# Attention outputs of three head groups in four copied by ScalarE, divided by GpSimd, and a re-timed order of work

## The reference, cut to what matters

```python
# second layer, causal
scores = jnp.einsum('bhqd,bhkd->bhqk', q, k) / np.sqrt(HEAD_DIM)
scores = jnp.where(causal, scores, -jnp.inf)
attn = jax.nn.softmax(scores, axis=-1)
out = jnp.einsum('bhqk,bhkd->bhqd', attn, v).transpose(0, 2, 1, 3).reshape(b, t, D_MODEL)
return out @ Wo.T
# third layer, two score entries set to -1e9
scores = jnp.einsum('bhqd,bhkd->bhqk', q, k) * scale
scores = scores.at[:, :, 0, -1].set(NEG)
scores = scores.at[:, :, -1, 0].set(NEG)
weights = jax.nn.softmax(scores, axis=-1)
out = jnp.einsum('bhqk,bhkd->bhqd', weights, v)
```

## Time and profile before

| | |
|---|---|
| median of 3 runs | 982.8 us (980.64 to 985.89) |
| the profiled execution | 983.22 us, span 981.6 us |
| PE busy | 876.7 us (89%) |
| DVE busy | 763.0 us (78%) |
| ACT busy | 654.7 us (67%) |
| POOL busy | 354.1 us (36%) |
| chain that ended last | PE 35%, DVE 12%, ACT 5%, issue 3% |

### The profile page before, as it was taken

One profiled execution on the slowest core, in us unless ns is written; L12 is line 12 of the kernel. 1 busy time (PEld: TensorE's weight loads), 2 busy tenths in 40 slices (PEclk: granted clock), 3 DMA queues, 4 the chain that ended last, 5 costly groups with the idle time before them and its releaser, 6 DMA issues.

```text
span 981.6 us, 22916 instructions
## 1 busy us (share of the span) xinstructions
PE 876.7 (89%) x9121; PEld 443.7 (45%) x9127; DVE 763.0 (78%) x1156; ACT 654.7 (67%) x1285; POOL 354.1 (36%) x575
## 2 busy tenths in 40 slices
PE   7999899999878989986889689979989999999985
PEld 5777777778522444443563222326322222222232
DVE  5676676866587778887568599866889999999855
ACT  2556556666336867875556568655778888999972
POOL 1543667567342642235255112432451112111340
PEclk9999999999899999999998999989999999999999
DMA  8000000200501143121420620033106000100000
GB/s 307 1 2 2 1 2 1 76 1 2 155 4 40 35 146 120 37 59 53 120 73 2 189 59 24 12 104 94 53 2 208 21 21 21 38 4 2 5 23 22
DMA packets 49597, 52.52 MB, mean 54 GB/s; under 512 B 9066, under 2 KB 40810, under 8 KB 49332
## 3 DMA queue, kind: packets, MB, share of 16 engines
q1 hardware_dynamic: 45204, 48.12, 16.3%
q0 software_dynamic: 4288, 2.94, 1.1%
HBM read 32.37 MB, written 19.68 MB: 53 GB/s over the span
## 4 chain that ended last, share of the span: by engine, by line
PE 35%; DVE 12%; ACT 5%; issue 3%; DMA 1%; POOL 1%; another core or an unknown queue 1%; DVEq 0%; ACTq 0%; SPq 0%; POOLq 0%
PE banks L1692 12%; PE banks L1657 8%; DVE arena L2031 8%; PE banks L1577 5%; ACT arena L1851 3%; PE banks L1767 2%; PE banks L1775 2%; PE banks L1700 1%; PE banks L1788 1%; PE banks L1715 1%; DMA arena<-arena 1%; ACT arena L1864 1%; DVE arena L2028 0%; PE banks L1811 0%
## 5 line engine op out<-in xcount | busy, mean ns | idle before, releaser
L2031 DVE TENSOR_REDUCE arena<-banks 128x2 f32<-128x1024 f32 (+1 forms) x384 | 441.3, 1197 | 58.0 <-PE banks L1577 28.9
L1851 ACT ACTIVATE arena<-banks 128x512 f32<-128x512 f32 (+1 forms) x768 | 409.8, 588 | 95.4 <-PE banks L1657 64.0
L1692 PE MATMUL banks<-arena 128*9 128x256 f32 (+1 forms) x3328 | 251.2, 381 | 6.7 <-ACT arena L1864 3.9
L1657 PE MATMUL banks<-arena 61*128 61x512 bf16 (+4 forms) x896 | 165.7, 370 | 32.6 <-ACT arena L1851 17.1
L1577 PE MATMUL banks<-arena 56*128 56x512 bf16 (+3 forms) x896 | 163.2, 367 | 20.5 <-DVE arena L2031 15.0
L1657 PEld LDWEIGHTS banks<-arena 61*128 61x128 bf16 (+1 forms) x896 | 44.0, 93 | 192.7 <-ACT arena L1851 157.6
L1433 POOL CAST arena<-arena 16x128 bf16<-16x128 f32 x32 | 9.0, 281 | 293.2 <-ACT arena L1919 283.7
L1692 PEld LDWEIGHTS banks<-arena 128*9 128x9 f32 x3328 | 52.9, 89 | 134.0 <-issue 83.2
L1577 PEld LDWEIGHTS banks<-arena 56*128 56x128 bf16 x896 | 45.2, 95 | 43.4 <-DVE arena L2031 33.3
L414 POOL TENSOR_TENSOR arena<-arena 128x8 f32<-128x8 f32 (+1 forms) x35 | 50.3, 1439 | 30.0 <-DVE arena L2195 27.6
L1443 POOL DMA_DIRECT2D arena<-arena x96 | 55.2, 579 | 10.8 <-POOL arena L1436 9.3
(11 more groups left out here) (241 smaller groups left out, 1398.0 us busy)
## 6 DMA issues: line engine op xcount, KB each, us to landing
arena<-k_products SPq DMA_DIRECT2D x32, 224.0 KB
arena<-q_products SPq DMA_DIRECT2D x64, 112.0 KB
arena<-e_w SPq DMA_DIRECT2D x22, 256.0 KB
q_products<-arena SPq DMA_DIRECT2D x12, 384.0 KB, 3.3
k_products<-arena SPq DMA_DIRECT2D x12, 384.0 KB, 3.9
arena<-arena POOLq DMA_DIRECT2D x96, 4.0 KB, 1.8
sorted_rows<-c_pads SPq DMA_DIRECT2D x2, 709.5 KB, 8.5
q_products<-arena SPq DMA_DIRECT2D x4, 288.0 KB, 3.9
```

What stands on the lines that cost most here:

```text
L1657: ins = nc.tensor.matmul(bank(S_BANK + (use + par) % SCORES)[:, at:at + C - o], Ks[n % NS][rows, y, kt * P:(kt + 1) * P], Qs[n % NS][rows, ...
L1692: ins = nc.tensor.matmul(PS[h * VROWS:h * VROWS + VW, AV_BANK, o:end], V[:, b, kt, HG * g + h, :], Pr[u % PROBS][:, h, o:end], start=(kt = ...
L1851: s_.activation(Pr[s % PROBS][:, 2 * x + par, o:C], scores[:, o:C], ACT.Exp) \
L2031: v_.tensor_reduce(of[:, :, x], two_banks[:, :, 0:width], AX.X, ALU.max).then_inc(ring_dve, 1)
```

## The change

For the first three head groups of each batch and layer (24 of the 32 blocks), the event `O` becomes `Oa`. PE's four transposes stay. ACT copies the 16 x 9 columns from the bank to a new tile `kept`; DVE does nothing. After the third group, a new event `den` has DVE take the reciprocals of all three groups' sums at once (8 times 48 columns), and POOL multiply three groups into `On` (8 times 384 columns). The fourth group keeps the old way. `N` on PE also waits for POOL's multiply. POOL gets one wait more ahead of an early event (`ln3`).

Besides, the table `MOVED` is replaced: about a hundred events move by half a unit to one and a half units against before. A second table moves the scans of units 3, 17, 18, 39 and 125 to 127 by one unit. A third adds two idle matmuls of 512 columns ahead of the first transposes of the experts (`h`, batch 0, tile 4).

```diff
+SCANS_MOVED = {3: -1, 17: 1, 18: 1, 39: 1, 125: 1, 126: 1, 127: 1}
+WARMED = {('h', (0, 4)): 2}
...
+    "H": {(0, 0): 0.5, (0, 1): 0.5, (1, 0): 0.5, (1, 1): 0.5},
...
+    "M": {4: 0.5, 5: -0.5, 7: -0.5, 13: -0.5, 14: -0.5, 15: -1, 21: 0.5, 29: -0.5, 30: -0.5},
...
+        kept, kept_den = A.tile(2, QT, AH - HG, AD + 1), A.tile(2, QT, AH - HG)
...
+        def turned(m):
+
+            return "O" if m // 2 % NG == NG - 1 else "Oa"
...
-                after.setdefault(end + 1 + o_lag, []).append(("O", m))
+                after.setdefault(end + 1 + o_lag, []).append((turned(m), m))
+                if m // 2 % NG == NG - 2:
+                    after.setdefault(end + 2 + o_lag, []).append(("den", (m // 2 // NG, m % 2)))
...
+                    elif kind == "den":
+                        b, c = k
+                        pool.wait_ge(den_ready, 2 * b + c + 1)
+                        g_.tensor_tensor(On[:, QT * c:QT * (c + 1), 0:P - HG * AD].rearrange("p t (h e) -> p t h e", e=AD),
+                                         kept[:, c, :, :, 0:AD],
+                                         kept_den[:, c].unsqueeze(3).to_broadcast([P, QT, AH - HG, AD]),
+                                         ALU.mult).then_inc(on_scaled, 1)
...
+                        pe.wait_ge(on_scaled, 2 * b + c + 1)
...
+                    elif kind == "Oa":
+                        n, c = divmod(k, 2)
+                        b, g = divmod(n, NG)
+                        act.wait_ge(ring_full, place[kind, k] + 1)
+                        if g == 0 and b:
+                            act.wait_ge(on_scaled, 2 * (b - 1) + c + 1)
+                        o4 = bank(ring_bank(place[kind, k])).rearrange("p (t h e) -> p t h e", t=QT, h=HG)
+                        s_.activation(kept[:, c, :, HG * g:HG * (g + 1), :], o4[:, :, :, 0:AD + 1], ACT.Copy) \
+                          .then_inc(ring_act, 1)
...
+                    elif kind == "den":
+                        b, c = k
+                        taken(dve, "Oa", 2 * (NG * b + NG - 2) + c)
+                        ready(dve, on_scaled, 2 * (b - 1) + c + 1)
+                        v_.reciprocal(kept_den[:, c], kept[:, c, :, :, AD]).then_inc(den_ready, 1)
```

More of the change, by code:

```diff
@@ L48 @@
 MOVED = {
-    "D": {1: -0.5},
-    "D17a": {15: 0.5},
-    "D17b": {15: 1},
-    "KS": {2: -0.5, 3: -0.5},
-    "M": {0: 1, 4: 0.5, 15: -1, 20: 0.5, 23: -1, 25: 1},
-    "N": {(0, 0): 0.5},
-    "O": {1: 1, 2: 1, 6: 1, 7: 1, 8: 1, 9: 1, 10: 1.5, 11: 1, 12: 1, 13: 1, 14: 1, 15: 1, 16: 1.5, 17: 1, 18: 1.5,
-        19: 0.5, 20: 1, 24: 1, 25: 1, 26: 1, 27: 1, 28: 1, 29: 1.5, 30: 1},
-    "Ta": {2: -0.5},
-    "Y": {(0, 0): -0.5, (0, 1): -1, (1, 0): -1, (1, 1): -0.5, (2, 0): -0.5, (3, 0): -0.5},
-    "k": {0: -0.5, 1: -0.5, 2: 0.5},
-    "k_part0": {4: -0.5},
-    "k_part1": {5: -1},
-    "k_part2": {5: -1, 7: 1},
-    "k_rem": {4: -0.5},
[14 rows of a table added]
+    "den": {(0, 0): -0.5, (0, 1): -0.5, (2, 0): 0.5, (3, 0): -0.5},
+    "k_part0": {5: 0.5, 6: 0.5, 7: 0.5},
+    "k_part1": {3: -0.5},
+    "k_part2": {2: 1, 3: -0.5, 7: 1},
+    "k_rem": {3: -0.5},
     "lat": {3: 1},
-    "ln": {3: 0.5},
+    "ln": {2: -0.5},
     "ln3": {3: 0.5},
-    "q": {0: -0.5, 1: -1},
-    "q_part0": {2: 0.5, 3: 0.5},
-    "q_part1": {3: 1, 5: -1},
-    "q_part2": {2: 0.5, 3: 0.5, 5: -0.5, 6: 0.5, 7: 1.5},
-    "q_rem": {4: -0.5},
-    "scale": {0: -1},
-    "split": {0: 0.5, 4: 0.5, 15: -1, 23: -1},
-    "square": {(0, 0): 0.5, (1, 0): -1},
-    "v": {1: -0.5, 2: 1, 3: 1},
-    "warm": {6: 0.5},
-    "x": {(0, 0): 0.5, (0, 1): 0.5, (0, 2): 0.5},
-    "xs3": {3: -1},
-}
+    "put": {(1, 1): -0.5, (1, 2): -0.5},
+    "q": {0: -0.5},
+    "q_part0": {2: 0.5, 6: 0.5, 7: 0.5},
+    "q_part1": {4: -0.5},
+    "scale": {2: 0.5, 3: 1},
+    "split": {4: 1.5, 5: -0.5, 7: -0.5, 15: -1, 21: 0.5, 27: 1, 29: -0.5},
+    "square": {(0, 0): 0.5, (1, 0): -1, (1, 1): 1},
+    "stat": {(1, 0): -0.5, (1, 1): -0.5},
+    "warm": {2: 0.5, 6: 1},
+    "x": {(0, 2): -0.5},
+}
+SCANS_MOVED = {3: -1, 17: 1, 18: 1, 39: 1, 125: 1, 126: 1, 127: 1}
+WARMED = {('h', (0, 4)): 2}
 SORTED = NT + NE - 1
@@ L389, in build @@
                                          "k_full", "k_part0", "k_rem", "k_part1", "k_part2")}
+        den_ready, on_scaled = sem("denominators_inverted"), sem("first_groups_scaled")
         counts = {}
@@ L1091, in scanned, with lead_of @@
         def scanned(u):
+            return lead_of(u) + SCANS_MOVED.get(u, 0)
+        def lead_of(u):
             if u < AHEAD:
@@ L1200, in order @@
                           ("warm", 20), ("Ta", 3), ("warm", 2), ("P", 3), ("R", 3)]
-        RINGED = "A M O N Y W T Ta P H G C x h y D k q v T0 Q QS lat KL K KS V0".split()
-        BY_ACT, BY_BOTH = "M H x k q Ta T0 Q QS lat KL K KS V0".split(), "h"
+        RINGED = "A M O Oa N Y W T Ta P H G C x h y D k q v T0 Q QS lat KL K KS V0".split()
+        BY_ACT, BY_BOTH = "M Oa H x k q Ta T0 Q QS lat KL K KS V0".split(), "h"
         ring = [e for e in order() if e[0] in RINGED]
@@ L1417, in _ @@
                     elif kind == "ln3":
+                        pool.wait_ge(av_cleared, 1)
                         t = slice(QT * k, QT * (k + 1))
@@ L1539, in _ @@
                             pe.wait_ge(o_kept if q >= 2 else g_silu, NTILE)
+                        warm(bk, WARMED.get((kind, k), 0))
                     if kind == "D16a":
@@ L1642, in _ @@
                             pe.wait_ge(exp_done, exps_of[use + 1 - SCORES])
+                        warm(bank(S_BANK + use % SCORES), WARMED.get((kind, k), 0))
                         if x == 0 and kt == 0:
@@ L1696, in _ @@
                             ins.then_inc(av_done, 1)
-                    elif kind == "O":
+                    elif kind in ("O", "Oa"):
                         pe.wait_ge(o_copied, k + 1)
```

2 lines of the change are left out of this document (1 added, 1 removed), and 11 rows, old and new, of the table MOVED.

## The result

| | before | after |
|---|---|---|
| median | 981.5 us | 973.3 us (969.9 to 977.9) |
| ratio | | 0.991, 95% interval 0.9892 to 0.9929 |
| profiled execution | 983.2 us, span 981.6 | 972.5 us, span 970.7 |
| mean granted clock of it | 0.975 | 0.981 |

The change makes the kernel 0.9% faster, 8.2 us by the medians. The two profiled executions differ by 10.9 us of span, and a part of that is not the change: over 40 executions of the kernel before on the same chip, the mean granted clock of TensorE went from 0.966 to 0.985, and the times at these two ends are 987.4 and 975.8 us, 6.1 us for each 0.01; a straight line fitted through all 40 gives 5.7. By these slopes the 0.006 between the two profiles go along with 3.4 to 3.7 us.

A forecast was written before the change was run, and what follows sets the result against it. DVE was taken as nearly full in 280 us behind the retention, PE close behind. DVE -5.3, ACT +2.0, moves -4.2 and reload +1.1 gave -6.4 from 983.2: 976.8 us, likeliest 972 to 979, 8-in-10 range 968 to 986.

The forecast's parts named there:

- DVE's relief: At the 24 `O` taken off DVE, 0.61 us each: -2.2, -2.1 and -1.0 us on the path.
- ACT's price: 24 copies of 0.37 us on ACT: +1.0 us in blocks 24 to 28, +1.0 us at the other 19 places.
- `den` on DVE: Eight new reciprocals of 48 columns at 0.27 us each give 2.2 us of work back to DVE.
- GpSimd's product: Eight new 384-column products on POOL, at most 1.27 us each: nothing on the path, even with a split queued behind.
- The moved events: Waits at block 0's start, `KL` 2, block 5, `H` and block 25, 6.35 us together: two thirds go, -4.2 us.
- the prediction's own sign of being wrong: Wrong if the waits turn up again one event later, or if unpriced moves carry more than 3 us.
- The rest: The other moves and the later scans 125 to 127: taken as zero, with 3 us to either side.
- The reload: `q_part2` 5 half a unit later, so PE's 2.26 us wait for the reload at 553.64 grows: +1.1 us.
- no change: PE and ACT take over from DVE and waits return at the next event: 982 us, chance 0.25.
- All of it: DVE's 12.4 us count nearly in full and the moved events' waits go: 970 us, chance 0.12.
- ACT in the loop: All 24 copies delay the exponentials, 8.9 us on the path, hiding DVE's relief: 989 us, chance 0.10.
- POOL against DVE: Eight POOL products each hold one DVE instruction by 1.4 us, 11.4 us in all: 988 us, chance 0.03.

The follow-up runs named there:

- Experiment 4: Changed kernel, with DVE given a 16-column reciprocal and a 128-column sum at each of the 24 copied outputs: 972.54 us, ratio 0.9918.
- experiment 5: Changed kernel, with ScalarE doing each of the 24 copies twice, the first into an unread tile: 971.82 us, ratio 0.9904.
- Experiment 1: Changed kernel's new `O` with the old table of moves, no moved scans, no idle matmuls: 988.75 us, ratio 1.0081 to the kernel before.
- experiment 6: Kernel of experiment 1 with two `den` later, behind splits 22 and 31 (the second also behind block 29's copy): 982.87 us, ratio 1.0025.
- experiment 3: Kernel before, old `O`, with only the moves that the prediction priced: 980.21 us, ratio 0.9992.
- experiments 2: Changed kernel's table, moved scans and idle matmuls, but every `O` the old way on DVE: 975.77 us, ratio 0.9944.
- experiment 7: Kernel before, old `O`, with the new table's 57 changed entries ahead of unit 96, scans 3, 17, 18, 39 moved, and idle matmuls: 973.75 us, ratio 0.9928.
- experiment 10: Kernel before with four table entries changed around unit 76 (`O` 11, `M` 13, `M` 14, `scale` 0): ratio 0.9977, on another chip.
- experiment 8: Kernel of experiment 1 with idle matmuls on PE in the two waits for splits, blocks 22 and 31: 989.55 us, ratio 1.008.
- e9: Changed kernel with `q_part2` 7 (the last reload) one and a half units later: ratio 0.9902, 959.4 us beside 970.4 on another chip.
- e12: Kernel before, old `O`, with the 29 changed entries ahead of unit 28 and moved scans 3, 17, 18: ratio 0.9961, on another chip.

## Why the prediction came near, and where its steps failed

The time, 973.3 us, lies 3.5 us under the forecast of 976.8 and inside its range. The mechanism was wrong, and the sum came near by luck: wrong terms cancelled.

*DVE's relief, -5.3 us in three terms: nothing that can be measured.* Experiment 4 gives DVE the time back at no cost. The step that failed is the reading of the earlier trace rows. The wait of 0.34 us ahead of the scan product was charged to the `O`. Its releaser is a scan, and that scan stands ahead of the reciprocal in DVE's queue. DVE's scans and the reciprocal behind them, in the kernel before (PE's weight load follows at 850.17):

```profile
847.77 2.35 DVE L2031 TENSOR_REDUCE arena<-banks 128x2 f32<-128x1024 f32 x2
...
850.04 0.25 DVE L2043 RECIPROCAL arena<-banks 128x16 f32<-128x16 f32 x1
```

The same place in the kernel after, without any `O` on DVE:

```profile
838.27 2.35 DVE L2068 TENSOR_REDUCE arena<-banks 128x2 f32<-128x1024 f32 x2
...
840.24 0.30 ACT L1949 ACTIVATE arena<-banks 128x144 f32<-128x144 f32 x1 [0.27 <-PE banks L1727]
...
840.67 0.10 PEld L1603 LDWEIGHTS banks<-arena 56*128 56x128 bf16 x2 [0.34 <-DVE arena L2068]
...
841.17 1.23 DVE L2068 TENSOR_REDUCE arena<-banks 128x2 f32<-128x1024 f32 x1 [0.55 <-PE banks L1608]
```

The wait is 0.34 us again, and the half unit 1.37 us again (840.24 to 841.61), not 1.14 to 1.3. DVE now stands idle 0.55 us where it did the `O` before. A stretch in which DVE works 97% of the time can still have room where the instruction stands.

*ACT's price, +2.0 us: nothing that can be measured* (experiment 5). The same rows show the copy starting in ScalarE's idle time. Its length was 0.30 us, between 0.27 and 0.60 as bounded, under the 0.37 taken, and the next instruction starts before it ends (840.42 here, 0.18 us behind the copy's start). The Trainium skill's figure ("VectorE: DVE Perf Modes", the section on the TRN2 errata) gave an estimate of 0.26 us; the measured 0.30 is nearer to it than to the row that the prediction took.

*`den` on DVE* took 0.45 us, not 0.27: two rows of 16 and 128 columns don't price a reciprocal of 48. 3.6 us of DVE instead of 2.2, hidden.

*GpSimd's product, nothing on the path: right only for the new table.* The step named the mishap ("behind it in POOL's queue can stand a block's split, which would be late by 1.3 us at most") and priced it at nothing, as the DMAs had several units. Experiment 1 measured 1.2 us late and 2.54 us of waiting, since the late DMAs fell in with the reload, and two places with what followed cost 5.9 us by the medians (7.7 us in units 128 to 222 of the two profiles, experiment 6). The new table puts split 22 and the copy of block 29 ahead of their `den`. The structure and its table had to be priced together.

*The moved events, -4.2 us for five named waits: the sign right, the reason short.* In the kernel after 5.2 us net of the 6.35 are gone, and at `KL` 2 the prediction's own sign of being wrong is there: the wait turned up again one event later, 1.17 us ahead of `K` 2. The named moves alone brought 0.8 us (at most 2.8, experiment 3). *The rest "zero, with 3 us to either side"* was the larger term: the start as a whole brings 3.8 us, `O` 11 and its neighbours another 2.2, and the whole table 5.5 to 7.1 (experiments 2 and 7), so the unpriced moves carry more than 3 us. The wait of 2.88 us at 517.18 is longer than any of the earlier trace rows and was not among them, though the diff moves `O` 11. And waits were priced by their length alone, without the clock behind them.

*The reload, +1.1 us: wrong in sign.* PE's wait for it went from 2.26 to 0.55 us, with 1.40 us for a split just ahead of it, 1.95 together, where 3.4 was expected.

Of the rivals, *no change* and *all of it* both rested on DVE. *All of it* also has its sum wrong: it says that DVE's 12.4 us count nearly in full and puts in 8; with 12.4 it would be 965.5 us, outside its own 966 to 972. *ACT in the loop* fell by experiment 5. *POOL against DVE* didn't occur at the new product. One line on the 32 merges of the kernel after and one on the eight products, durations in ns as least, median and most:

```profile
L2075 DVE TENSOR_TENSOR arena<-arena x32: 175/176/1041, 265.8 to 915.3; 128x16 f32<-128x16 f32 x32
```
```profile
L1448 POOL TENSOR_TENSOR arena<-arena x8: 849/854/1164, 374.0 to 916.0; 128x384 f32<-128x384 f32 x8
```

The three long merges lie beside other two-tile instructions of GpSimd (at 353.11, 434.83 and 504.65 us); the one long product, at 525.66, lies beside DVE's product of `q_rem`. So instructions of the two engines take longer side by side, as the earlier trace rows showed, and either engine can be the one held, but no merge met the new product. The merge reads two SBUF tiles, as in the rule that the prediction cites from the Trainium skill ("GPSIMD Engine Reference", section 8), and this trace agrees: up to 1.04 us beside GpSimd instead of 0.18.

## What to carry to other kernels

Before crediting an instruction with a wait, look where the releaser stands in its queue: work that stands behind the releaser can be taken away at no gain, however full the engine. Put the old cost back by itself: one run that gave DVE its work back told more than the sum of all DVE's terms. When an operation is split over a second engine, list what stands behind each new wait on that engine, DMAs that feed another engine first, and price structure and order together.

## What the runs showed of the hardware

The place of PE's idle time counts, not only its sum. Behind a wait of 2.88 us at 517 us and one of 2.54 us at 754 us the granted clock was 0.50 for 5 us and more, and work took up to 1.94 us instead of 1.12; behind a single wait of 1.53 us at 746.7 us half units stayed at 1.12. Cut in two (experiment 10) or filled with idle matmuls (experiment 8), the wait left the clock at 1.00. But the same wait at the same place can go either way. Behind the 1.39 us that PE waits for a scan at 717.96 us in the kernel before and at 711.30 in experiment 7, the windows are:

```profile
718.00:721.00 3.00, 3.00 (x33) 1.21 (x35) 2.90 (x7) 1.31 (x3) 1.30 (x4) 1.00 0.00 0
711.00:714.00 3.00, 2.70 (x17) 1.09 (x19) 1.93 (x4) 0.29 (x2) 0.36 (x2) 0.54 0.00 0
```

So one profile doesn't tell whether a wait costs the clock. The spread of the kernel before from run to run, 975.8 to 988.0 us, goes along with the mean granted clock.

The three DMAs of split 22 had landed 4.8 us after the first was issued when the reload came 1.2 us behind them (experiment 6), and 5.9 to 6.1 us after it when the reload was issued in the same moment (experiment 1 and the kernel after). Those of split 31, with no reload beside them, took 3.1 us (experiment 1). On another chip the kernel before took 970.4 us instead of 981, and the stages that were shorter there are two beside the experts, units 96 to 127 (114.3 to 114.9 us in e9 to e12, 119.3 to 121.8 in the profiles of the first chip) and units 56 to 71 (65.7 and 65.8 in e12 and e10, but 68.1 in e9). In the first of them PE stands still for 3.28 us at 640.68 in the kernel before, and nothing in the profile ends that wait; the kernels on the other chip don't have it. Why is open.
